# A graph-attention layer with layer norm: the scores on four quarters of TensorE, and the low parts of the relu blocks earlier on VectorE

## The reference, cut to what matters

```python
adj = dep_type_matrix != 0
hi = h @ W1[:384] + emb(adj) @ W1[384:] + b1
hj = h @ W2[:384] + emb(adj) @ W2[384:] + b2
relevance = sum(hi * hj, axis=-1)                 # 64 x 64 scores of a graph
A = softmax(where(adj, relevance, -1e9), axis=2)
z = relu((A @ h) @ gcn_w + gcn_b)
y = x + z @ Wo + bo
out = (y - mean) / sqrt(var + 1e-5)
```

## Time and profile before

| | us |
|---|---|
| median of 3 runs | 373.93 (373.79 to 374.37) |
| the profiled execution, its own time | 374.34 |
| its span, first to last instruction | 372.5 |
| PE busy | 364.6 (98% of the span) |
| DVE busy | 274.7 (74%) |
| ACT busy | 179.9 (48%) |
| POOL busy | 145.0 (39%) |
| one body of the loop, mix to mix | 21.92 |

### The profile page before, as it was taken

One profiled execution on the slowest core, in us unless ns is written; L12 is line 12 of the kernel. 1 busy time (PEld: TensorE's weight loads), 2 busy tenths in 40 slices (PEclk: granted clock), 3 DMA queues, 4 the chain that ended last, 5 costly groups with the idle time before them and its releaser, 6 DMA issues.

```text
span 372.5 us, 9938 instructions
## 1 busy us (share of the span) xinstructions
PE 364.6 (98%) x3827; PEld 317.0 (85%) x3827; DVE 274.7 (74%) x773; ACT 179.9 (48%) x371; POOL 145.0 (39%) x108
## 2 busy tenths in 40 slices
PE   8998999999999999999999999999999999999994
PEld 5787898988889898898989889898988989888993
DVE  1559868687786868788586777858677785867955
ACT  1665717164272725528272561826346181625562
POOL 1603561716135171523517152261714326141814
PEclk9999999999999999999999999999999999999998
DMA  7995115564442556344355534435543444550033
GB/s 237 342 334 168 39 12 175 169 187 135 141 163 90 177 169 183 105 158 163 94 183 169 178 93 157 159 117 183 169 158 113 131 160 141 171 171 4 2 128 129
DMA packets 43268, 55.48 MB, mean 149 GB/s; under 512 B 10352, under 2 KB 37488, under 8 KB 43248
## 3 DMA queue, kind: packets, MB, share of 16 engines
q1 hardware_dynamic: 42448, 54.30, 46.0%
q10 hardware_dynamic: 800, 0.90, 0.7%
HBM read 42.61 MB, written 12.58 MB: 148 GB/s over the span
## 4 chain that ended last, share of the span: by engine, by line
PE 90%; DMA 3%; SPq 2%; DVE 2%; ACT 1%; issue 0%; POOL 0%; DVEq 0%
PE banks L463 27%; PE banks L465 26%; PE banks L464 25%; PE banks L517 7%; PE banks L483 6%; DMA wo_sb<-in_wo_w_dram 3%; SPq L382 1%; SPq L396 0%; ACT prob L752 0%; ACT wo_hi L745 0%; SPq L389 0%; SPq L392 0%; DVE at_sb L943 0%; DVE rel L955 0%; SPq L393 0%
## 5 line engine op out<-in xcount | busy, mean ns | idle before, releaser
L1132 POOL TENSOR_TENSOR y_sb<-y_sb,wob_sb 128x1536 f32<-128x1536 f32 x15 | 52.8, 3522 | 87.8 <-DVE y_sb L864 73.8
L764 ACT CAST z_hi<-banks 128x512 fp32r<-128x512 f32 x48 | 26.5, 588 | 97.8 <-PE banks L517 92.1
L842 DVE TENSOR_TENSOR y_sb<-banks,y_sb 128x384 f32<-128x384 f32 x60 | 33.4, 556 | 47.3 <-PE banks L465 43.7
L464 PE MATMUL banks<-wo_lo,hs_hi 128*128 128x384 f32 x180 | 60.5, 336 | 0.0
L463 PE MATMUL banks<-wo_hi,hs_hi 128*128 128x384 f32 x180 | 60.5, 336 | 0.0
L465 PE MATMUL banks<-wo_hi,hs_lo 128*128 128x384 f32 x180 | 60.5, 336 | 0.0
L463 PE MATMUL banks<-z_hi,gcn_hi 128*128 128x512 f32 x144 | 58.3, 405 | 0.0
L463 PE MATMUL banks<-xt_hi,m_hi 128*128 128x512 f32 x144 | 57.2, 397 | 0.0
L465 PE MATMUL banks<-xt_hi,m_lo 128*128 128x512 f32 x144 | 56.5, 392 | 0.0
L465 PE MATMUL banks<-z_hi,gcn_lo 128*128 128x512 f32 x144 | 56.4, 392 | 0.0
L464 PE MATMUL banks<-z_lo,gcn_hi 128*128 128x512 f32 x144 | 56.1, 389 | 0.0
(11 more groups left out here) (103 smaller groups left out, 613.5 us busy)
## 6 DMA issues: line engine op xcount, KB each, us to landing
x_sb<-in_x_dram SPq DMA_DIRECT2D x16, 768.0 KB, 4.6
xt_sb<-in_x_t_dram SPq DMA_DIRECT2D x15, 768.0 KB, 6.5
y_sb<-in_x_dram SPq DMA_DIRECT2D x15, 768.0 KB, 4.6
out_dram<-y_sb SPq DMA_DIRECT2D x30, 384.0 KB, 2.5
adj_sb<-in_adj_dram SPq DMA_DIRECT2D x32, 64.0 KB, 3.0
xt_sb<-in_x_t_dram SPq DMA_DIRECT2D x2, 384.0 KB, 6.5
xt_sb<-in_x_dram SPq DMA_DIRECT2D x1, 768.0 KB, 6.1
w2t_sb<-in_w_t_dram SPq DMA_DIRECT2D x3, 192.0 KB, 4.4
```

Source lines behind the costliest of these rows:

```text
L464: pe.matmul(acc, a_hi, b_lo, start=False, stop=False)
L764: act.copy(by_graph(z_hi[:, f, :]), mixed(f)).then_inc(zhi, 1)
L842: dve.tensor_tensor(y_home(g, slot)[:, q, :], out_bank(g, q)[:, 0:HID], y_home(g, slot)[:, q, :], ALU.add).then_inc(added, 1)
L1132: pool.tensor_tensor(y_home(g, slot), y_home(g, slot), wob_sb[:].rearrange("p (o n) -> p o n", o=1).to_broadcast([P, PAIRS, HID]), ALU.add ...
```

## The change

Two edits, and what they need. First, each of a pair's score products is cut along its 128 rows into two halves of 64, so that `score_stage` issues 48 fp32 products on quarters of the array, in the same form as `mix`. The two row halves may not add in one bank, so they go to banks 0 and 2 (`SCORE_BANK`), and VectorE adds the two: one operation over 128 x 256 adds the row term and the first bank, one the second bank, one multiplies by the mask; before there were four operations of 128 x 64 that added and multiplied at once. The banks of `gemm`, of `proj(1)` and of `out` change places so that bank 2 is free in time, and waits change with them (a new semaphore `summed`; `mix` waits for the residual of pair 1). Second, `low_hidden(g-1)` stands directly behind the transposes in bodies 2 to 14 as well, ahead of `row_products` and `normalise`.

```diff
-        GEMM_BANK = [bank[2], bank[3], bank[1]]
         score = bank[0]
+        SCORE_BANK = bank[0], bank[2]
+        GEMM_BANK = [bank[3], bank[1], bank[2]]
-        PROJ1_BANK = bank[1:4]
+        PROJ1_BANK = [bank[1], bank[3], bank[2]]
...
             def score_stage(g, par):
-                pe.wait_ge(gt_ready, C * (g + 1))
+                if static(g, 0) or static(g, 1):
+                    pe.wait_ge(gt_ready, C * (g + 1))
                 for n in range(PAIRS):
                     for c in range(C):
-                        for e in range(2):
-                            ts = slice(n * P + e * NODES, n * P + (e + 1) * NODES)
-                            mm = pe.matmul(score[e * NODES:(e + 1) * NODES, n * NODES:(n + 1) * NODES],
-                                           gt_sb[:, c, ts], xt_sb[:, par, c, ts], start=(c == 0), stop=(c == C - 1))
+                        for r in range(2):
+                            rows = slice(r * NODES, (r + 1) * NODES)
+                            for e in range(2):
+                                ts = slice(n * P + e * NODES, n * P + (e + 1) * NODES)
+                                mm = pe.matmul(SCORE_BANK[r][e * NODES:(e + 1) * NODES, n * NODES:(n + 1) * NODES],
+                                               gt_sb[rows, c, ts], xt_sb[rows, par, c, ts],
+                                               start=(c == 0), stop=(c == C - 1))
                 mm.then_inc(score_mm, 1)
...
             def gemm(g):
-                    elif not (static(g, 0) or static(g, LAST - 1) and f == C - 1):
-                        pe.wait_ge(added, PAIRS * (g - 1) + f + 2)
+                    elif f == C - 1:
+                        pe.wait_ge(summed, 2 * (g + 2))
+                    elif not (static(g, 0) or static(g, LAST - 1) and f == 1):
+                        pe.wait_ge(added, PAIRS * (g - 1) + f + 3)
...
             def mix(g, par):
                 elif not static(g, LAST):
                     pe.wait_ge(gt_ready, C * (g + 2))
+                    pe.wait_ge(added, PAIRS * (g - 1) + 2)
...
                 dve.wait_ge(score_mm, g + 1)
+                dve.wait_ge(srow_ready, g + 1)
+                first, second = (b[:, 0:MIX].rearrange("p (q n) -> p q n", n=NODES) for b in SCORE_BANK)
+                dve.tensor_tensor(rel[:], first, srow[:].rearrange("p (q o) -> p q o", o=1).to_broadcast([P, PAIRS, NODES]),
+                                  ALU.add).then_inc(summed, 1)
+                dve.wait_ge(summed, 2 * g + 1)
+                dve.tensor_tensor(rel[:], second, rel[:], ALU.add).then_inc(summed, 1)
+                dve.wait_ge(summed, 2 * g + 2)
                 dve.wait_ge(negm, g + 1)
-                dve.wait_ge(srow_ready, g + 1)
-                for q in range(PAIRS):
-                    a = dve.scalar_tensor_tensor(rel[:, q, :], score[:, q * NODES:(q + 1) * NODES],
-                                                 srow[:, q:q + 1], adj_sb[:, par, q, :], ALU.add, ALU.mult)
-                a.then_inc(masked, 1)
+                dve.tensor_tensor(rel[:], rel[:], adj_sb[:, par], ALU.mult).then_inc(masked, 1)
...
                 turn(g)
-                if static(g, 1):
+                if not (static(g, 0) or static(g, LAST)):
                     for f in range(C):
                         low_hidden(g - 1, f)
...
-                if not (static(g, 0) or static(g, 1)):
-                    for f in range(1 if static(g, LAST) else 0, C):
+                if static(g, LAST):
+                    for f in range(1, C):
                         low_hidden(g - 1, f)
```

More of the change, by code:

```diff
@@ L250, in gnn_layernorm_kernel @@
         srow_ready = sem("srow_ready")
+        summed = sem("summed")
         masked = sem("masked")
@@ L315, in out_bank @@
             if static(g, LAST - 2) and HALVES <= q:
-                return bank[(3, 2)[q - HALVES]]
+                return bank[3]
             if static(g, LAST - 1):
-                return bank[(3, 1, 6, 7)[q]]
+                return bank[(1, 2, 6, 7)[q]]
             if static(g, LAST):
-                return bank[(3, 1, 2, 4)[q]]
+                return bank[(1, 2, 3, 4)[q]]
             return bank[(1, 2, 3, 1)[q]]
         def gemm_bank(g):
-            return [bank[2], bank[4], bank[5]] if static(g, LAST) else GEMM_BANK
+            return [bank[3], bank[4], bank[5]] if static(g, LAST) else GEMM_BANK
         def column(g, q):
@@ L612, in body @@
                 if static(g, 0):
-                    proj(1, 1, PROJ1_BANK, range(2, C * C))
+                    proj(1, 1, PROJ1_BANK, range(2, 2 * C))
+                    pe.wait_ge(summed, 2)
+                    proj(1, 1, PROJ1_BANK, range(2 * C, C * C))
                     return
```

## The result

The changed kernel takes **385.88 us** (median of 5 runs, 385.13 to 386.32) against 373.93: the ratio is 1.0305, with a 95% interval of 1.029 to 1.032. It is slower, as forecast, but by 11.95 us and not by 5.9, which lies outside the range. The profiled execution took 385.13 us with a span of 383.2; before it was 374.34 and 372.5. So 10.7 us of span have to be found; the profiled execution is the shortest of the five, and the other 1.2 us to the 11.95 of the medians are spread that it doesn't show.

What follows compares the result with a forecast made beforehand. TensorE, busy for 98% of the span, was taken to bound the kernel. Terms 2.1 + 2.2 + 1.1 + 0.5 = 5.9 us on the profiled 374.34 gave 380.2, or 379.8 against the median; range 374.8 to 383.

Steps and rivals of the forecast that it cites:

- The loop's body: Bodies 2 to 13: 22.10 us each in place of 21.92, +2.2 us in all.
- M+19.7: Start of VectorE's first residual, 19.7 us after the body's mix starts (M), having waited for GpSimd's bias.
- Body 1: VectorE's addition of `neg_sb` is held up beside GpSimd's `split_x`; +2.1 us with body 0's 0.50 in it.
- Body 14, +1.1: The mix after body 14 newly waits for the residual of pair 1: M+21.45 instead of M+20.36, +1.1 us.
- Body 15, +0.5: The last `out` of group 13 waits for the first low part, which hangs on the scores' chain: +0.5 us.
- The start, +0.50: In body 0 TensorE already waits for the transposes, so VectorE's three dependent sums cost it 0.50 us.
- Twice as many quarters in the same time: cutting them wins nothing in the stream: Scores on TensorE: the mix's 96 quarters take 1.63 us, the scores' 48 halves 1.62; no gain within the stream.
- The seam: Between mix and scores on TensorE, where the array changes from 64x64 to 128x64: 0.15 us saved per body.
- Behind it everything is the same, shifted: After body 15's last `out` of group 13, the rest of the kernel only moves later, at no further cost.
- the third: Rival: quarters don't stream as in the mix; scores take 3.1 us, the kernel 396 us; chance 0.03.

Runs made afterwards that it cites:

- the test of the third low part: Changed kernel with the third low part of the relu blocks behind the row products in bodies 2 to 14; 382.36 us, ratio 1.0218.
- the shifted code: Changed kernel with 16 more one-column matmuls in the warm-up, ahead of everything on TensorE; 389.23 us in the profiled execution.
- the bias set free: Changed kernel with GpSimd's bias waiting for the row products instead of for the normalise; 423.58 us, ratio 1.1286.

## Why the prediction failed

- **The loop's body: right.** Forecast 22.10; 22.11 measured (nine from 121.65 to 320.68). The forecast reason, M+19.7 for the residual and the bias ahead of it, is in the rows and passed the test of the third low part. Twelve bodies are 2.33 us of the 3.26, against a term of 2.16.
- **Body 1: right**, 1.60 for 1.59, by the addition held up.
- **Body 14, +1.1: right in mechanism and size.** With quarters and sums but no stop, in the shifted code, it is 21.54 against 20.36, 1.18 more, and its mix waits for the residual. The changed kernel's other 0.59 are a stop.
- **Body 15, +0.5: right as well**, 0.48 without a stop (11.57 against 11.09); the other 0.88 are a stop.
- **The start, +0.50: right in size.** From the first scores to the mix it is 8.01 us now. In the three runs with body 0 of before it is 7.49 to 7.51, so the sums cost some 0.51. The profiled execution of before took 7.79, because VectorE waited there for ScalarE's row term, which it doesn't in the others. VectorE's first score operation, before and with the low parts alone moved (first scores at 22.18 and 22.23):

```profile
24.14 0.86 DVE L955 SCALAR_TENSOR_TENSOR rel<-banks,srow,adj_sb 128x64 f32<-128x64 f32 x4 [2.95 <-ACT srow L719]
```

```profile
23.90 0.86 DVE L955 SCALAR_TENSOR_TENSOR rel<-banks,srow,adj_sb 128x64 f32<-128x64 f32 x4 [2.65 <-PE banks L483]
```

  The other 0.38 of the start's 0.89 is that wait and the time ahead of the first scores. They began at 21.88 to 22.95 in executions of the same code up to there, the 22.18 of before among them, so I count it as no effect of the change.
- **The step that failed is "Twice as many quarters in the same time: cutting them wins nothing in the stream".** It read the mix's 14 ns a quarter as a property of TensorE alone and asked nothing of the supply: a mix is 96 in a row; mix and scores are now 192. On first passes, in bodies 3, 14 and 15, the supply fell behind. Together the stops cost 2.4 us (0.93 of the 3.26 in bodies 2 to 13, 0.59 and 0.88). The seam itself closed: scores 1.45 us after the mix's start, 1.56 before, 0.11 saved of the forecast 0.15.
- **"Behind it everything is the same, shifted": wrong**, 1.83 us, the last store behind an instruction fetch.

So the terms of the forecast, each measured where no stop covers it, are 0.51 + 1.60 + 2.33 + 1.18 + 0.48 = 6.1 us for 5.9. The two things that it put at nothing gave 2.4 and 1.83. With the 0.38 of the start these are the 10.7 us of span. The prediction looked at waits and operations, and at no place in the page's own third part, where the instruction packets stand. Of the rivals, none named it; the third was right that a stream of quarters can be slower than the mix's, but for another reason: in bodies 4 to 13 it is not.

Open: how a piece of code is called for and how many lie ready, where the account of the places goes by counts alone, and why the fetch at the end comes 1.0 us after the store's issue in the changed kernel and 1.8 before.

## What to carry to other kernels

Cutting products into more and smaller ones may cost something even where they stream as fast. Where a hand-written stretch or a loop's first pass runs once, count its instructions per us, and look for instruction packets beside a stop called "issue". A stop that moves with code put ahead of it is told from a wait for data in one run. An operation moved ahead of another on one engine moves everything queued behind it on others too; follow the queue to where it returns, and compare with the slack there to the tenth of a us. And an order that keeps two engines apart, like the wait for `y_ready`, may be worth more than the idle time that it shows.

## What was unexpected of the hardware

- Instructions come by DMA during the run, some 16 KB at a time (15 packets, 0.25 MB), and TensorE went on 2.2 to 2.6 us after such a packet in three of three stops. It stood still 0.97 to 1.20 us each time (0.55 to 1.55 in the other runs, and 2.66 once with the bias set free) in a row of quarters, and in no scores on halves here.
- With such a fetch in the middle of a store, 9 of the store's 144 packets came some 1 us behind the others, and it took 4.0 us. With the fetch behind it, it took 1.9 to 2.2.
- A normalise of VectorE with one input in SBUF, 1.65 us for four, took 8.06 beside 7.6 us of GpSimd's work, which wasn't slowed at all.
